# The mean of squares of a head: four products in column tiles, the root on a quarter of the width, DMAs that spread it

## What is computed

```python
o = o * jax.lax.rsqrt(jnp.mean(o * o, -1, keepdims=True) + EPS)   # mean over the DH = 128 numbers of a head
o = o * o_norm_w * jax.nn.silu(gg)
return o.reshape(B, L, KEY_DIM) @ Wo.T
```

## Time and profile before

| what | value |
|---|---|
| median of 3 runs | 1228.02 us (1227.23 to 1228.38) |
| profiled execution, its time | 1221.33 us |
| profiled execution, span from first to last instruction | 1219.5 us |
| mean granted TensorE clock | 0.986 |
| busy in the span: PE, DVE, ACT, POOL | 1145.7, 814.1, 716.0, 499.3 us |

### The profile page before, as it was taken

One profiled execution on the slowest core, in us unless ns is written; L12 is line 12 of the kernel. 1 busy time (PEld: TensorE's weight loads), 2 busy tenths in 40 slices (PEclk: granted clock), 3 DMA queues, 4 the chain that ended last, 5 costly groups with the idle time before them and its releaser, 6 DMA issues.

```text
span 1219.5 us, 30002 instructions
## 1 busy us (share of the span) xinstructions
PE 1145.7 (94%) x12192; PEld 790.1 (65%) x12192; DVE 814.1 (67%) x1454; ACT 716.0 (59%) x1212; POOL 499.3 (41%) x709
## 2 busy tenths in 40 slices
PE   7888899999999999999998989859999999999987
PEld 2444455555555555555555556649998998998976
DVE  4897667768768768668576665665665566655552
ACT  3776467677677676776775866624444434445433
POOL 1659576575675774773774811100011000001000
PEclk9999799999999999999998999989999999999999
DMA  3123222323323223243326422161111122111100
GB/s 118 46 52 79 66 52 60 107 58 72 87 58 93 68 73 77 77 128 89 91 73 150 151 62 72 47 235 45 44 45 49 50 52 70 44 44 48 30 17 10
DMA packets 134602, 88.07 MB, mean 72 GB/s; under 512 B 79264, under 2 KB 118048, under 8 KB 133568
## 3 DMA queue, kind: packets, MB, share of 16 engines
q1 hardware_dynamic: 133312, 85.93, 25.9%
q10 hardware_dynamic: 1152, 0.21, 0.1%
HBM read 54.77 MB, written 14.55 MB: 57 GB/s over the span
## 4 chain that ended last, share of the span: by engine, by line
PE 75%; POOL 8%; DVE 5%; issue 4%; ACT 3%; SPq 2%; DMA 2%; ACTq 0%; POOLq 0%; DVEq 0%
PE proj L467 20%; PE out L1494 5%; PE turned_v_chain L1494 5%; PE gram L482 4%; PE turned_v_chain L1560 4%; PE proj L1552 4%; PE proj L1433 4%; POOL inverse L1204 3%; POOL rank_one L1201 3%; PE out L491 2%; PE turned_v_chain L596 2%; PE gram L1468 2%; PE decays L497 2%; PE turned_v_chain L629 2%; DVE conv L992 2%
## 5 line engine op out<-in xcount | busy, mean ns | idle before, releaser
L992 DVE SCALAR_TENSOR_TENSOR conv<-proj,kq_weights,conv 128x504 f32<-128x504 f32 (+2 forms) x261 | 189.9, 731 | 24.4 <-ACT conv L736 17.7
L467 PE MATMUL proj<-xT,vg_weights 128*128 128x512 f32 x384 | 190.6, 620 | 1.8 <-DVE conv L992 1.6
L1791 POOL TENSOR_TENSOR rope<-rope_part,rope_part 128x512 f32<-128x512 f32 x32 | 40.0, 1271 | 364.8 <-DVE rope_part L1730 364.8
L992 DVE SCALAR_TENSOR_TENSOR conv<-proj,vg_weights,conv 128x504 f32<-128x504 f32 (+2 forms) x192 | 140.8, 734 | 44.9 <-ACT conv L736 40.0
L467 PE MATMUL proj<-xT,kq_weights 128*128 128x512 f32 x348 | 164.5, 599 | 0.2 <-DVE conv L992 0.2
L1204 POOL TENSOR_TENSOR inverse<-inverse,rank_one 128x30 f32<-128x30 f32 (+14 forms) x240 | 125.2, 522 | 18.8
L1201 POOL TENSOR_TENSOR rank_one<-inverse 128x30 f32<-128x30 f32 (+14 forms) x240 | 117.7, 490 | 15.9
L467 PEld LDWEIGHTS proj<-xT,vg_weights 128*128 128x128 f32 x384 | 68.4, 192 | 65.6 <-issue 59.8
L467 PEld LDWEIGHTS proj<-xT,kq_weights 128*128 128x128 f32 x348 | 62.4, 190 | 72.8 <-issue 70.3
L1569 ACT ACTIVATE rstd<-rstd 128x1 f32<-128x1 f32 x48 | 9.8, 203 | 142.6 <-DVE rstd L1677 142.6
L482 PEld LDWEIGHTS gram<-keys_q 128*64 128x64 f32 x896 | 57.6, 138 | 54.7 <-ACT keys_q L747 36.4
(11 more groups left out here) (244 smaller groups left out, 2464.0 us busy)
## 6 DMA issues: line engine op xcount, KB each, us to landing
kq_weights<-in_kq_w SPq DMA_DIRECT2D x32, 390.0 KB, 3.5
vg_weights<-in_vg_w SPq DMA_DIRECT2D x32, 390.0 KB, 4.0
o_scratch<-oT SPq DMA_DIRECT2D x32, 256.0 KB, 2.9
o_in<-o_scratch SPq DMA_DIRECT2D x16, 512.0 KB, 4.1
diagonal<-gram_decayed SPq DMA_DIRECT2D x128, 32.0 KB, 1.9
inverse<-inverse SPq DMA_DIRECT2D x32, 128.0 KB, 2.7
q_first<-rope SPq DMA_DIRECT2D x128, 32.0 KB, 1.9
q_second<-rope SPq DMA_DIRECT2D x128, 32.0 KB, 1.9
```

Source lines behind the costliest of these rows:

```text
L467: mm = e.matmul(bank(c, u)[:], w[:, (k * 3 + c % 3) * 128:(k * 3 + c % 3 + 1) * 128], xT[g][:, k, :], start=(k == 0), stop=(k == KD - 1))
L992: e.scalar_tensor_tensor(acc(c, u)[:, :, back:], src[:, :, 0:S - back], weights(c, u)[:, j:j + 1], acc(c, u)[:, :, back:], ALU.mult, ALU.a ...
L1791: e.tensor_tensor(turned[half][:].rearrange("p b r q -> p r b q"), parts[2 * half][:], parts[2 * half + 1][:], op).then_inc(s_turned, 1)
```

## The change

For units 0 to 21 (`by_rows`; their norms are finished in slots 11 to 32) the one product of 512 columns becomes four of 128 columns. Product j uses 32 columns of `ones_mean` and writes the means of tokens 128j to 128j+127 into partitions 32j to 32j+31, so the whole result takes 128 x 128 instead of 128 x 512. Ln and Exp work on that (`o_rs_quarters`, called rs4). Then SP issues four DMAs, each of which reads one partition (32j) and writes its 128 numbers to all 128 partitions of a quarter of `o_rs`. The new semaphore `d_rs` counts them. POOL waits for it before it multiplies by the gate, and does that now after `decayed_causal`. SP's store of a rotated key (kind KRS) moves behind these DMAs, into the next slot. Units 22 to 31 stay as they were.

```diff
--- before.py
+++ after.py
@@ -192,7 +192,7 @@
         vT = [t(f"vT{i}", [128, GB, S, NH]) for i in range(2)]
         Vn = t("V", [128, GB, DH])
         gate = [t(f"gate{i}", [128, GB, S]) for i in range(3)]
-        o_sum, o_rs = t("o_sum", [128, GT]), t("o_rs", [128, GT])
+        o_sum, o_rs, rs4 = t("o_sum", [128, GT]), t("o_rs", [128, GT]), t("o_rs_quarters", [128, TILE])
         n2, inv, rho, kln, kn = (t(n, [128, RB]) for n in ("n2", "inv", "rho", "k_ln", "k_norm_turned"))
         knorm = [t(f"k_norm{i}", [128, B]) for i in range(2)]
         room.close("rest")
@@ -228,6 +228,7 @@
 
         d_wab, d_small, d_ident, d_const, d_late, d_diag, d_inv = (sem(n) for n in (
             "d_w_ab", "d_small", "d_ident", "d_const", "d_late", "d_diag", "d_inverse"))
+        d_rs = sem("d_o_rs")
         d_x = [sem(f"d_x{i}") for i in range(NG)]
         d_pconst, d_pin, d_kv, d_pout, d_rope, s_pmm, s_pout, s_padd = (sem(f"prepare_{n}") for n in (
             "const", "in", "kv_stored", "stored", "rope_stored", "product", "copied", "rope"))
@@ -283,6 +284,7 @@
             if n > 0:
                 e.wait_ge(s, n)
 
+        by_rows = lambda u: u < U - LAG - 1
         PREPARE = LAG + 1
         KV, TOKENS, KR, KRS, QN, UVO = range(6)
 
@@ -388,6 +390,15 @@
                     e.dma_start(xT[g][:], a["xT"][:, :, g * GT:(g + 1) * GT]).then_inc(d_x[g], 16)
                 for s in range(SLOTS):
                     ua, ub, uc, uo = s, s - 1, s - LAG, s - LAG - 2
+                    if live(uo) and by_rows(uo):
+                        e.wait_ge(s_rs, uo + 1)
+                        wait(e, s_og, uo)
+                        for j in range(4):
+                            e.dma_start(o_rs[:, j * TILE:(j + 1) * TILE],
+                                        rs4[RB * j:RB * j + 1, None, :].broadcast_to([1, 128, TILE])).then_inc(d_rs, 16)
+                    rotated = prepare_at(s - 1)
+                    if rotated is not None and rotated[1] == KRS:
+                        prepare_store(*rotated)
                     if live(ua + 1):
                         wait(e, s_conv[Q], 3 * ua)
                         e.dma_start(blob_a[(ua + 1) % 2][:], a["kq_w"][head(ua + 1)]).then_inc(d_wa[(ua + 1) % 2], 16)
@@ -418,7 +429,7 @@
                                         (table[0], "cos64"), (table[1], "sin64")):
                             e.dma_start(tile[:], a[n]).then_inc(d_pconst, 16)
                     now, then = prepare_at(s), prepare_at(s + 1)
-                    if now is not None:
+                    if now is not None and now[1] != KRS:
                         prepare_store(*now)
                     if then is not None:
                         wait(e, s_pmm, then[0])
@@ -626,7 +637,13 @@
 
                 def norm(u):
                     e.wait_ge(s_osum, u + 1)
-                    e.matmul(VB, ones_mean[:], o_sum[:], start=True, stop=True).then_inc(s_norm, 1)
+                    if by_rows(u):
+                        for j in range(4):
+                            mm = e.matmul(VB[rows(j), 0:TILE], ones_mean[:, 0:RB], o_sum[:, j * TILE:(j + 1) * TILE],
+                                          start=True, stop=True)
+                    else:
+                        mm = e.matmul(VB, ones_mean[:], o_sum[:], start=True, stop=True)
+                    mm.then_inc(s_norm, 1)
 
                 for s in range(LAG + 1, SLOTS):
                     ua, ub, uc, ud = s, s - 1, s - LAG, s - LAG - 1
@@ -868,13 +885,18 @@
                         e.preload_act_table_set(LN_EXP)
                     if live(uo):
                         e.wait_ge(s_norm, uo + 1)
-                        wait(e, s_og, uo)
-                        e.activation(o_rs[:], VB, ACT.Ln, scale=float(2 ** O_SHIFT), bias=guard[:, 0:1]).then_inc(s_ln, 1)
+                        if by_rows(uo):
+                            wait(e, d_rs, 64 * uo)
+                            o_ln, o_mean = rs4[:], VB[:, 0:TILE]
+                        else:
+                            wait(e, s_og, uo)
+                            o_ln, o_mean = o_rs[:], VB
+                        e.activation(o_ln, o_mean, ACT.Ln, scale=float(2 ** O_SHIFT), bias=guard[:, 0:1]).then_inc(s_ln, 1)
                     if late_q:
                         tap(Q, ub)
                     if live(uo):
                         e.wait_ge(s_ln, uo + 1)
-                        e.activation(o_rs[:], o_rs[:], ACT.Exp, scale=-0.5).then_inc(s_rs, 1)
+                        e.activation(o_ln, o_ln, ACT.Exp, scale=-0.5).then_inc(s_rs, 1)
                     if s in rope_slots:
                         ahead["rsqrt"](0, rope_slots[s])
                     if s == last_slot + 1:
@@ -1249,13 +1271,12 @@
                     if s == 0:
                         e.wait_ge(d_const, 48)
                         e.wait_ge(s_gdve, 15)
-                    if live(uo) and s <= U:
-                        e.wait_ge(s_rs, uo + 1)
-                        e.wait_ge(s_silu[G], uo + 1)
-                        wait(e, s_og, uo)
-                        e.tensor_tensor(o_rs[:], flat(gate[uo % 3]), o_rs[:], ALU.mult).then_inc(s_gr, 1)
                     if live(ub) and s != LAG:
                         decayed_causal(ub)
+                    if live(uo) and s <= U:
+                        e.wait_ge(d_rs, 64 * (uo + 1))
+                        e.wait_ge(s_silu[G], uo + 1)
+                        e.tensor_tensor(o_rs[:], flat(gate[uo % 3]), o_rs[:], ALU.mult).then_inc(s_gr, 1)
                     if live(ud):
                         e.wait_ge(s_wloout, ud + 1)
                         e.wait_ge(s_solve, SOLVE * batch(ud) + K_NORM)
```

## The result

| | before | after |
|---|---|---|
| median | 1227.62 us (1226.05 to 1228.38, 4 runs) | 1389.03 us (1383.56 to 1392.41, 4 runs) |
| ratio | | 1.131, 95% interval 1.127 to 1.135 |
| span of the profiled execution | 1219.5 us | 1387.3 us |

What follows compares the result with a forecast made beforehand. PE was taken to bound slots 11 to 32. PE's saving -3.3, elimination +10.3 and queue +18.3 gave +25.3 on 1221.33: 1246.6 us for the profiled execution, median 1253, range 1236 to 1270.

Steps and rivals of the forecast that it cites:

- The step that failed: The four spreading DMAs, first issue to last landing: 3.8 us, bounds 3.25 and 4.7.
- The rival that had it: Slow copies from one partition: each us on the landing costs 11 us; at 6 us landing, 1277; chance 0.05.
- Queue term, 18.3: Slots 13, 17, 21, 25, 29: spreading waits behind the inverse's DMAs in SP's queue, oT late; 14.0 plus 4.3 us.
- 0.8 for diagonals and turns that come late: Queue slots: 0.4 for the two DMA groups' mean, 0.4 for DVE's lost slack; SP free at +8.6.
- Elimination term, 10.3: POOL's late gate product delays elimination, inverse and chain_low: 1.65 us in five slots, 2.05 in slot 32.
- wait over 2 us: Sign: the inverse's turn waits over 2 us for POOL at the end of slots 12, 16, 20, 24, 28.
- PE's part, 0.3 a slot: Four tiled products replace two passes before the q projection: 0.3 us saved a slot, bounds nothing and 0.65.
- the bound with all four tiles at once: PE's norm products: four column tiles fully parallel, 0.21 us, saving 0.65 a slot.
- The clock, rival with 0.17 and +8.5: PE's holes of 2 to 3.5 us halve its clock, 1.7 us in each of five slots; 1262; chance 0.17.
- only the queue costs: POOL's delay vanishes, six slots save 0.3 instead; only the queue slots lose: +13, 1241 us; chance 0.2.
- Faster: oT does not set slots 13 to 29, POOL's delay is covered, PE's saving remains: -6.6, 1221 us; chance 0.1.
- the moved KRS store, priced at nothing: Slots 14, 18, 22 and similar: earlier load delays spreading about 1 us, covered; 0, bound +0.5 in five slots.

Runs made afterwards that it cites:

- own_rows: The changed kernel, but each spreading DMA reads all 128 partitions of the quarter tile once, not one partition 128 times (values then wrong): 1259.8 us.
- inverse_behind: from_32_rows with the four DMAs of the inverse moved behind the next slot's spreading in SP's queue: 1245.2 us.
- from_32_rows: The changed kernel, but each spreading DMA reads the 32 partitions of its band four times each, not one partition 128 times: 1261.9 us.
- no_spread: The changed kernel without spreading DMAs; POOL multiplies the gate by the quarter tile, repeated four times (values wrong): 1225.9 us, ratio 0.998 to the kernel before.
- plain_only: from_32_rows, but only the 11 units whose norm ends in a slot without the inverse's turn or its DMAs take the new way: 1221.8 us, ratio 0.997.
- filled_4: The changed kernel with four extra PE products in slots 11 to 31, ahead of the place where PE waits for oT: 1376.6 us.

## Why the prediction was wrong

**The step that failed** is "From the first issue to the last landing: 3 x 0.5 + 2.3 = 3.8 us, bounds 3 x 0.45 + 1.9 = 3.25 and 3 x 0.69 + 2.6 = 4.7". The landings of the earlier trace rows are of DMAs whose partitions are all different; the sentence ahead of it, "No DMA of the trace reads one partition for 128", named the hole, and I still bounded the cost from both sides by rows that couldn't see it. It was 10.1 us. With the same DMAs on different partitions it was 4.0, inside my bounds. own_rows is therefore the kernel that I forecast: 1259.8 against 1253, inside the range. The remaining 129 us are the source. That it came so near is in part luck: its slots are 35.3 us longer in the profile, where I had 25.3, but its median does not lie 6.7 above the profiled execution, as I had taken over from the kernel before.

**The rival that had it** was given 0.05 and the wrong slope: "Each us on the landing costs 11 us". It costs 20 to 22. I had counted the 11 slots in which the slack was nothing already and left the plain ones as covered, however late. Their cover ends soon: at a landing of 4.0 they lose nothing, at 6.2 1.4 us each, at 10.1 5.6 each.

**Queue term, 18.3:** the mechanism was right, the size too small. own_rows 27.3, and inverse_behind takes 14.4 of what from_32_rows has (23.0) away. In slot 21, +5.2 where I had 3.5, the spreading is issued at +9.33, where I had +8.6, and `oT` starts at +14.6 (I had +13.85):

```profile
396.48 0.42 PE L642 MATMUL turned_v_chain<-o_sum,ones_mean 128*32 128x128 f32 x8
...
405.81 2.58 SPq L397 DMA_DIRECT2D o_rs<-o_rs_quarters  x4
...
411.08 0.75 DVE L1150 SCALAR_TENSOR_TENSOR oT<-out,o_norm_w,o_rs 128x512 f32<-128x512 f32 x1 [4.73 <-POOL o_rs L1279]
...
411.89 2.07 PE L465 MATMUL out<-prepare_kv,w_kr_swapped 64*128 64x512 f32 x2 [2.49 <-DVE oT L1150]
```

The last row shows what I had left out of the term: the clock, at half (2.07 for a product that takes 1.12 at full clock). The other part was there, but too small. I had added 0.8 for diagonals and turns that come late; the second half of the inverse's turn ends 0.4 later in the slot, and SP issues the diagonals from +2.8 instead of +2.4 and needs 3.59 instead of 2.57 for them, so the four DMAs behind them start 1.5 later and not 0.8.

**Elimination term, 10.3:** 12.4 in own_rows, with the row that I had named. In slot 20 DVE waits for the elimination, PE for `less_sum`:

```profile
392.49 2.05 DVE L1060 STREAM_TRANSPOSE inverse<-inverse 128x1024 f32<-128x1024 f32 x1 [3.33 <-POOL inverse L1308]
...
395.47 1.08 PE L607 MATMUL turned_v_chain<-kq_decayed,inverse 64*32 64x64 f32 x32 [2.44 <-DVE kq_decayed L1091]
```

I had "wait over 2 us" for the turn (3.33 against 0.33 in the earlier trace rows) and 1.65 a slot; the five slots have 1.9 on the mean. Without any landing they have 0.1 to 0.2 (no_spread, where PE's 0.5 is lost in them).

**PE's part, 0.3 a slot:** 0.51 in the untouched plain slots. From the first tiled product to the projection it takes 0.35 us, where 0.97 was the old figure, 0.65 my forecast from the pattern of two tiles, and 0.32 the bound with all four tiles at once. So the tiles overlap nearly as far as my bound had it; 0.1 is lost again, as the projection behind them takes 1.98 instead of 1.88. It makes 2 us of 161.

**The clock, rival with 0.17 and +8.5:** it fell in every kind of slot and not in five, for 157 of the stretch's 652 us, and for over 40 in own_rows already. In the changed kernel it is worth at least 12 us.

**The other rivals:** "only the queue costs" fell with own_rows (the turn slots lose 12.4). "Faster" fell with the landings: even without any DMA it is 1225.9. That plain_only reaches 1221.8, where this rival had 1221, is chance: 11 slots of 0.5 there, 22 of 0.3 here. And the moved KRS store, priced at nothing, has no trace in the plain slots of own_rows (18 and 22 are 0.5 shorter, as the others).

## What to carry to other kernels

A DMA that repeats its source is priced by where it reads, not by its size: here one partition, or four neighbours, gave 27 GB/s together, and reading copies that lie in 32 partitions made the same spreading 2.3 times as fast, for one changed index. Where the trace has no row for an access pattern, the nearest rows are no bounds; ask what the pattern shares that theirs doesn't. Slack is a threshold and not a yes or no: price a late step in every slot that it runs in, with the lateness at which each begins to pay.

## What the runs showed of the hardware

- 27 GB/s from one partition, 26 from four neighbouring ones, 99 from four that lie 8 apart; no more than 26 where a DMA from partition 0 meets one from 32, but 70 where 32 meets 64. The DMA engines looked busy at 0.69 meanwhile, with packets of 206 ns (27 ns in own_rows), so a busy DMA share can be a queue for one source.
- The slow packets held up others in the queue: `kq_weights` landed in 6.5 us instead of 3.5, and `vg_weights` in 6.1 instead of 4.0. No one waited for them for long.
- Four products of 128 columns in four column tiles of 32 took 0.35 us from their start to that of the next group, against 0.97 for the two passes of 512 columns that they replace.
- PE's clock fell to half around two holes of 3.21 and 1.66 us ahead of the projection in slot 19 of the changed kernel, and stayed full in the same slot of filled_4 with 1.21 ahead of it. A single hole of 3.24 (slot 29 of plain_only) left it full too, so the length of one hole alone doesn't tell.
